# Two lanes of a decoder's last stage: another order of the same steps on each engine

## The reference

```python
x = _layernorm(x + _L2_attn_ref(x, ...), axis=-1)     # long convolution, gated
x = _layernorm(x + _L2_xattn_ref(x, ctx_1024, ctx_1024, ...), axis=-1)   # cross attention, 16 heads
x = _layernorm(x + _L2_ffn_ref(x, L2_ffn_rhs), axis=-1)   # int8 product
x = _layernorm(x + _L3_attn_ref(x, ...), axis=-1)     # retention
x = _layernorm(x + _L3_xattn_ref(x, ctx_1024, mask_Bx1x1xS2_ff0, ...), axis=-1)  # cross, self attention, gelu layer
x = _layernorm(x + _L3_ffn_ref(x, ...), axis=-1)      # ternary products with silu and gelu
```

## Time and profile before

| | us |
|---|---|
| median of 3 runs | 3095.99 |
| the 3 runs | 3096.03, 3090.25, 3095.99 |
| the profiled execution | 3092.62 |
| its span, first to last instruction | 3090.8 |
| the last stage in it | 1554 to 3090.8 |
| end of the last product of the last round | 3079.2 |

### The profile page before, as it was taken

The page is one execution under the profiler, slowest core; times in us unless marked ns, Lnnn a source line. Parts: engine busy times, 40 slices in busy tenths (PEclk is TensorE's granted clock), DMA queues, the critical chain, the costliest instruction groups (busy, mean ns, idle before and its releaser), DMA issues.

```text
span 3090.8 us, 47481 instructions
## 1 busy us (share of the span) xinstructions
PE 2391.3 (77%) x20196; PEld 1589.6 (51%) x20196; DVE 1694.6 (55%) x4103; ACT 1040.4 (34%) x1534; POOL 357.9 (12%) x605
## 2 busy tenths in 40 slices
PE   4665478887888887787678779777797777887788
PEld 2433256666666665665545454444454444544444
DVE  5776736556665663531358651675417753447641
ACT  4464212222322231012132542434423344334442
POOL 0111000011001000036111000110001100111000
PEclk9887568878978887988788999899898899999999
DMA  2000000000000000212710000000000000000000
GB/s 89 1 1 3 1 1 8 1 8 8 8 1 8 8 1 8 102 24 34 175 64 1 1 8 1 1 1 1 8 0 1 1 1 4 4 1 1 1 1 28
DMA packets 39335, 47.80 MB, mean 15 GB/s; under 512 B 7170, under 2 KB 36370, under 8 KB 38355
## 3 DMA queue, kind: packets, MB, share of 16 engines
q1 hardware_dynamic: 33490, 40.43, 4.4%
q0 software_dynamic: 5632, 4.33, 1.1%
HBM read 31.82 MB, written 12.91 MB: 14 GB/s over the span
## 4 chain that ended last, share of the span: by engine, by line
PE 57%; DVE 25%; ACT 8%; issue 4%; POOL 3%; DMA 1%; SPq 0%; DVEq 0%; another core or an unknown queue 0%; POOLq 0%; ACTq 0%
PE banks L2604 7%; DVE wide_area L2477 4%; PE banks L1279 3%; PE banks L1489 2%; DVE wide_area L1891 2%; PE banks L920 2%; PE banks L2353 2%; PE banks L1454 2%; PE banks L1522 2%; PE banks L2362 2%; PE banks L948 2%; PE banks L2372 2%; PE banks L1802 1%; PE banks L1788 1%; PE banks L2591 1%
## 5 line engine op out<-in xcount | busy, mean ns | idle before, releaser
L2477 DVE TENSOR_REDUCE wide_area<-banks 128x8 f32<-128x2048 f32 x64 | 146.7, 2292 | 106.2 <-PE banks L2353 106.0
L2456 ACT ACTIVATE weights<-banks 128x2048 f32<-128x2048 f32 x64 | 120.0, 1877 | 128.4 <-PE banks L2362 128.3
L1007 POOL TENSOR_TENSOR rstd<-moments,eps 128x4 f32<-128x4 f32 x56 | 11.9, 212 | 1208.5 <-DVE moments L996 1208.5
L991 DVE BATCH_NORM_STATS2 stats<-banks 128x6 f32<-128x128 f32 x208 | 50.3, 287 | 181.3 <-PE banks L959 100.1
L1891 DVE TENSOR_REDUCE wide_area<-banks 128x16 f32<-128x1024 f32 x80 | 94.3, 1217 | 44.3 <-PE banks L1788 44.2
L1279 PE MATMUL banks<-wC,weights 128*128 128x72 f32 x512 | 84.7, 343 | 18.3 <-ACT weights L1328 18.3
L991 DVE BATCH_NORM_STATS2 dilvals<-banks 128x6 f32<-128x128 f32 x144 | 35.2, 287 | 113.6 <-PE banks L959 85.0
L1279 PEld LDWEIGHTS banks<-wC,weights 128*128 128x128 f32 x512 | 81.8, 255 | 26.3 <-ACT weights L1328 26.3
L1021 PE MATMUL banks<-wA,xs 128*128 128x128 f32 x208 | 49.2, 335 | 59.1 <-DVE xs L1000 58.2
L1000 DVE TENSOR_SCALAR xs<-banks,moments,rstd 128x128 f32<-128x128 f32 x208 | 70.6, 401 | 37.0 <-POOL rstd L1009 36.8
L2604 PE MATMUL banks<-wide_area,big 128*128 128x512 f32 x192 | 87.0, 595 | 0.0
(11 more groups left out here) (776 smaller groups left out, 6273.0 us busy)
## 6 DMA issues: line engine op xcount, KB each, us to landing
big<-in_wE SPq DMA_DIRECT2D x1, 4096.0 KB, 12.8
weights<-long_kernel SPq DMA_DIRECT2D x8, 512.0 KB, 7.5
conv<-wide_area SPq DMA_DIRECT2D x16, 256.0 KB, 3.0
wC<-in_wC SPq DMA_DIRECT2D x1, 3012.0 KB, 17.3
wC<-in_wG SPq DMA_DIRECT2D x1, 2971.0 KB, 19.3
big<-in_wT SPq DMA_DIRECT2D x1, 2560.0 KB, 11.3
x_all<-in_xT SPq DMA_DIRECT2D x1, 2048.0 KB, 10.9
total<-spread SPq DMA_DIRECT2D x8, 256.0 KB, 2.3
```

The source lines that it names most:

```text
L991: dve.bn_stats(m.stats[:, i, :], self.tokens(i)).then_inc(*sg.up("dve", f"stats{i}"))
L2456: act.activation(m.weights, bank[:, :, :].rearrange("p r c -> p (r c)"), ACT.Exp, scale=DK ** -0.5)\
L2477: return dve.tensor_reduce(m.peaks[:, k % 2, :, :].rearrange("p t (r c) -> p r t c", r=4)[:, :, :, SPARE[j]], m.bank[:, :, :].rearrange("p ...
```

## The change

The four strings of `ORDERS["last"]` are replaced by four others of the same length, with as many n and f each. No instruction is added, removed or altered, and the tables of the other stages stay. The strings of before and after agree over long parts: of the 1216 steps on PE that raise a semaphore of a lane, 417 stand in 134 short pieces whose order differs; on DVE it is 466 of 1992 in 65 pieces, on ACT 215 of 784 in 68 pieces, on POOL 20 of 232 in 4.

```diff
@@ ORDERS["last"] @@
-        "pe": "nnffnnnfnnnnnffffffnfnnfnnfnffnfnfnnnfnnffnffnffffnnnnnnnnnnffffnfffffffnnnnnnnnnfffnfffffffnnfnfnfnfnffnnfffffnfnnffnff"
+        "pe": "nnffnnnfffnnnnnffffnfnnfnnfnffnfnfnnnfnnfffnfffffnnnnnnnnnnffffnfffffffnnnnnnnnnffffnffffnfnfnffnfnfnnfffnffffnfnnffnnf"
...
-        "dve": "nnffnnnfffnnfnnfnfffnnnnnnffffffnnnnnnfffnfffnfnfnnfnnnffnfffnnfnfffnnffnnfffnnffffnfnnffnnnnffnfnfnfnnnfnnffnnnfnnffffn"
+        "dve": "nnnffnnfffnnfnnfnfffnnnnnnffffffnnnnnnfffffnfnfnfnnfnnnffnfffnnfnfffnnffnnffffnnffffnnfnnfnnnfffnffnnnnnfnnffnnfnnfffnfn"
...
```

More of the change, by code:

```diff
@@ new lines @@
+        "act": "nnnfffnnnnnfffffnnnnnfffffnnnnnnnnfffffnffffnnnnnnffffffnnnnnnfffnnfffffnnffnnffffnnffffnfnnnnnffffnnnnfnfnnnnnfffffnnnn"
+             "nfffffnnnnnnnnffffffnfffnnnnnnnfffffffnnnnffffnnnnffffnnnnffffnnnnffffnnnnffffnnnnffffnnnnffffnnnnfffnnnfnffffnnnnnnnnff"
+             "ffffffnnnnnnnnnnnnnnnnnffffnfffffnnffffnnnffnnfnnnfnfnnnnnnfffffffnnnnnnffffnnnfnnnfffnnnffnnnnnnnnffffffffnnfnnnnffffff"
+             "nnffnnfnfffnfnnnfnnffnnnnffnffnnnnffnfffffffnnnnfnnnnfnnnnnnfffnnffnnnfffnffnnnffffnfffffnnnnfffffffnnnnffffnnnnffffnnnn"
+             "ffffnnnnffffnnnffffnnnnnffffnnnnnnnnffffffffffffnnnnnnnnnffffnfffnfnnnnfffffnnffnffffffnnfnfffnnfnnfffffnnnffnnfffffnnnn"
+             "nfffffnnnnnnnnnffffnnffnnnnfffnnfffnffnfnnnnffnnffffnnffnnffffnnnnnffnffnnffnnnnnfnfnnfffnnnnnffnnnnnfffnnnffnnnnnnnnfff"
+             "ffnnnnfffffnnnfffnfffnnnffnfffnnnnffffnnnnffffnnnnffffnnnfffnfnnnnnnnnfffnnfnnnnnnffffnnnnnfffnnnnnnnnnnnnnfnnnnnnnffffn"
+             "nfffnnnfnnnnfffffnfffnnnnnnnnnfffffffffnnnnnfnfffffnnfffnnnnnnfffffffnnfffffnnnnnnfffnnfnnfnnfffffnnfnfffffffffnnnnnffff"
+             "ffffnnnnnfffffffffffnnnnnffffnnnffnnnnffnnnnfffnnnnfffffnnnnfffffffffnnnnfffffffnnnnffffnnnnffffnnnnffffnnnnffffnnnfffnn"
+             "nnfnfffnnfnnnnnnffffffffnnnnnfffnnnfnnfffffnfnfnfnnffffnfnfffffffffffnffnnffnf",
@@ L862 @@
+        "pool": "fnnfnnffnnnnnnnnnnnnffffffffffffnnnnffffnnnfffnnnnnnnnnnnnnnnnffffffffffffffffnnnnnnnnnnnnnnffffffffffffffnnnnnnnnnnnnnn"
              "nnnnnnnnnnnnnnnnnnnnnfffffffffffffffffffffffffffffffffffnnnnnfffffnnnnnnnnnnnnnfffffffffffffnnnnnnnnnnnnnnnnnnnfffffffff"
-             "ffffffffffnnnnnnnnnnnnnnnnnnnnnnnnnnnnffffffffffffffffnnffffffffffffffnnnnnnnnnnnnnnnnnnnnnnnnnnnnnnnnnnnnnnnnffffffffff"
+             "ffffffffffnnnnnnnnnnnnnnnnnnnnnnnnnnnnffffffffffffffnnffffffffffffffffnnnnnnnnnnnnnnnnnnnnnnnnnnnnnnnnnnnnnnnnffffffffff"
```

39 lines of the change are left out of this document (20 added, 19 removed).

## The result

The change made the kernel slower by a third of a percent. Over 20 runs each, its median is 3095.41 us against 3087.65 us of the kernel before, 7.8 us more. The ratio estimated from all of them is 1.0033 (95% interval 1.0020 to 1.0047), some 10 us (6 to 15). Two of the three runs shown of the kernel before were at the upper end of its own spread (3074.17 to 3096.35), and the third lay above its median. One later run, of e10, took 3693.22 us at a granted clock of 0.613 and is left out everywhere. The result is inside the forecast's range, but on the other side of no change.

What follows compares the result with a forecast made beforehand. PE was taken as full in the ternary layer and paced by lane chains in self attention. Terms of -5.4 and -3.1 made -8.5 us, 3084.1 on the profiled run, 3087.5 as median, range 3073 to 3102.

Steps and rivals of the forecast that it cites:

- What bounds the kernel: Last stage: PE full in the ternary layer, each lane's chain sets the pace in self attention, 9.80 us a unit.
- Places 1 and 2: Ends of the two lanes' self attention in round 2: shorter waits, forecast -3.9 us together.
- place 2: Round 2, far lane's last self-attention unit: peak and query go ahead, -2.9 us; near lane's 3.2 us slip hidden.
- Place 1: Round 2, near lane's last self-attention unit: turned scores right behind the far lane's scores, -1.0 us, at most -1.45.
- Starts of cross attention: Rounds 1, 2 and 4: far lane's context products ahead of a norm's transposes, -0.8 us, between 0 and -1.6.
- Starts of self attention: Rounds 2 and 4: far lane's key masks moved ahead of a near-lane step, -0.2 and -0.7 us.
- the rest: Over a hundred small pieces, mostly swaps of neighbours, not priced singly: -3.1 us, bounded by +5 and -11.
- The end: After the last sum: the near lane's norm shares DVE with the far lane's, +0.2 us, between 0 and +1.4.
- The clock: PE's time at 1.2 GHz in the last stage: set at zero, though a fifth more or less is 15 us.
- slower by the clock: Rival: mixed stretches fall to 1.2 GHz; 50 us more there gives +11.5 us, so 3107; slower had 19%.
- Absorbed: Rival: gains are lost at the lanes' next meeting and small pieces cancel, 0 to -6 us, about 3093; 31%.
- The level: Whole kernel: profiled run lies 3.4 us under the shown runs' median 3095.99; same difference on the median gives 3087.5.

Runs made afterwards that it cites:

- e10: The kernel before with the new order only at places 1 and 2 and in two stretches of round 4; ratio 0.9974 to the kernel before, -8 us.
- e1: The kernel before, run again with no edit; ratio 1.0011 to the kernel before, -0.7 us at an equal clock.
- e8: The kernel before with the new order at places 1 and 2 and in four stretches of rounds 3 and 4; ratio 0.9947, -16 us.
- e4: The kernel before with the new order at places 1 and 2 alone; ratio 0.9988, -3.7 us, at an equal clock -2.2.

## Why the prediction was wrong

**What bounds the kernel.** Right. The losses found are waits of PE between the lanes; the plain self-attention periods kept their 9.80 us.

**Places 1 and 2, -3.9 us.** The sum isn't contradicted (-3.7 by the runs' ratio, -2.2 at an equal clock), and the order of events at place 2 was right to 0.1 us. Place 1 brought 0.1 to 1.5 us where I had 1.0. Place 2 was mis-sized: 0.4 us arrived at the near lane's ternary layer where I had 2.9. The named cover, the far lane's next transposes, did not hide the near lane's norm, which slipped by 5.4 us and not 3.2.

**Starts of cross attention, -0.8 us.** Not tested alone. In round 1 the move removed 0.67 us of wait, and the next L1795 and L1788 waited 0.57 and 0.77 us more. Over the first 80 us of the stage the four traces with the new order there take 77.5 to 78.7 us and the ten with the old one 79.4 to 80.6, but with 7 to 10 us less at 1.2 GHz, which by the prices above is worth as much or more. So no gain of the order itself is shown.

**Starts of self attention, and "the rest".** This is the step that failed. I had -0.9 us for two of the four starts, from a single move of key masks in each, and put everything else into "over a hundred pieces" at -3.1, bounded by +5. The four starts cost +8.4 us (+1.5 to +15), measured alone, and at an equal clock the rest cost 5.0 more. (A tenth of the 33 us is also 3.3 and not 3.1.) The reason for the miss is in how I looked: I searched the trace for steps that were ready and stood behind one that was not, which finds only gains. A new order also puts ready steps behind late ones, and that can be read from the same trace. In round 1 (times of e1's trace, whose order is that of before) L1859 could only start at 1710.61, when PE needed L1863's output at 1710.47. Exchanging them puts L1863's end at about 1711.6, a wait of some 1.1 us; 1.08 came. This is one wait, worked out once its result was known. I think that a second search in that direction would have taken the negative sign off the rest; that isn't shown.

**The end, +0.2 us.** The tail is 4.95 us as before, so 0. The 5.1 to 5.5 us that I called "as now" was a misreading: it was 4.95 then too.

**The clock, set at zero.** The mean of the last stage in the changed kernel's trace is 0.95, inside the band. The price of a microsecond at the lower level is 0.29 us over the whole kernel, where I had up to 0.4; in the stretches of rounds 3 and 4 above it was 0.4 to 0.5. The rival "slower by the clock" gave the right side with the wrong mechanism: over the whole kernel the changed one spends no more time at the lower clock (809 us against 826), and is slower by its waits. Its 3107 was also too far.

**Absorbed.** What is won is indeed given back at place 2 and in round 3 of e8. But as a whole the change did not end at zero.

**The level.** I set the forecast from 3 runs, whose median lay 8 us above that of the 20 that came in the end. Two errors of 8 and 16 us cancelled in part, which is why 3087.5 looks closer than it was.

## What to carry to other kernels

When a change only reorders, walk the trace in both directions: for each moved step ask whether it was ready behind a late one, and for each step that is moved behind another ask when that other one's input came. Small swaps where a phase begins, with all engines passing steps between two lanes, made most of the half-microsecond waits here, though not all of them. The orders of the engines fit each other: one engine's new order without the others' can cost as much as all. And don't compare two profiles by their spans when the clock moves: compare stretches between common points at full clock, or correct the runs by their clock.

## What the runs showed of the hardware

The same steps in the same order can take 83.3 or 99.5 us. Round 1 between the same two steps of PE, in the kernel before again (e1) and in e4, whose order is the same until round 2:

```profile
1622.40:1705.70 83.30, 61.97 (x718) 38.55 (x721) 66.18 (x156) 25.96 (x47) 8.90 (x12) 0.96 0.00 1
```

```profile
1626.30:1725.80 99.50, 82.87 (x718) 49.48 (x722) 66.60 (x155) 25.93 (x47) 8.91 (x12) 0.71 0.00 1
```

The granted clock is 0.96 in one and 0.71 in the other, 7 against 58 us at 1.2 GHz, and DVE, ACT and POOL are busy for the same time. The Trainium skill (TensorE: Matmul & The Clock Gate, What's actually happening) calls the activity window free-running, so that the same work can fall differently into it; these two rows agree. Over whole runs of one kernel the time at the lower clock has a standard deviation of 13 to 33 us, and the span one of 4 to 9 us. I had not expected how exact the rest is: at full clock the start of self attention in round 2 takes 24.84 to 24.86 us in seven traces of the old order, from three chips, in a kernel of 3090 us.
